# A two-layer perceiver kernel: its first loads split and reordered, and ScalarE's first instruction put ahead of its waits

## The reference, cut to what matters

```python
x = x + _L0_xattn_ref(_layernorm(x), ctx_1024, ctx_1024, ...)   # cross attention, 16 heads, causal
x = x + _L0_attn_ref(_layernorm(x), ...)                        # gated self attention with a position bias
x = x + _L0_ffn_ref(_layernorm(x), ...)                         # feed-forward with quantized weights and values
x = x + _L1_xattn_ref(_layernorm(x), ctx_1024, ctx_1024, ...)   # cross attention over all 257 context tokens
x = x + _L1_attn_ref(_layernorm(x), ...)                        # self attention with a line bias
x = x + _L1_ffn_ref(_layernorm(x), ...)                         # three-layer feed-forward
```

```python
def _L0_xattn_ref(queries, keys, values, Wq, bq, Wk, bk, Wv, bv, Wo, bo):
    q = (queries @ Wq.T + bq).reshape(N, L, H, -1)
    k = (keys @ Wk.T + bk).reshape(N, S, H, -1)
    v = (values @ Wv.T + bv).reshape(N, S, H, -1)
    sm = jnp.einsum('nlhd,nshd->nlhs', q, k) / math.sqrt(D)
    causal_mask = jnp.triu(jnp.ones((L, S), dtype=bool), k=1)
    sm = jnp.where(causal_mask[None, :, None, :], -jnp.inf, sm)
    sm = jax.nn.softmax(sm, axis=-1)
    attn = jnp.einsum('nlhs,nshd->nlhd', sm, v)
    return attn.reshape(N, L, H * D) @ Wo.T + bo
```

## Time and profile before

| what | us |
|---|---|
| median of three runs | 1635.74 (1635.74 to 1636.04) |
| the profiled execution | 1634.2 |
| its span, first to last instruction | 1632.4 |
| TensorE busy in the span | 1463.9 (90%) |
| VectorE / ScalarE / GpSimd busy | 897.7 / 712.2 / 498.9 |

### The profile page before, as it was taken

How to read it: one execution, slowest core, us unless ns; L and a number is a source line. 1 busy time by engine, 2 the same in 40 slices (tenths; PEclk the granted TensorE clock), 3 DMA queues, 4 the chain that set the end, 5 groups by cost and what they waited for, 6 DMA issues and landing times.

```text
span 1632.4 us, 32837 instructions
## 1 busy us (share of the span) xinstructions
PE 1463.9 (90%) x12556; PEld 1127.3 (69%) x12556; DVE 897.7 (55%) x1896; ACT 712.2 (44%) x1761; POOL 498.9 (31%) x693
## 2 busy tenths in 40 slices
PE   3998996991799999999996688789999999999999
PEld 3887774431677777777775466548877885886787
DVE  3898897488545555565655588734224323422332
ACT  3887775395535554555553455421212211221221
POOL 1445551001026865865553577500000000000000
PEclk9999999995999999999998799989999999999999
DMA  7000000000031161145110000013321440342230
GB/s 280 24 10 2 1 0 1 1 0 27 14 130 40 39 237 46 39 142 211 39 32 2 1 2 0 1 45 136 135 104 50 153 159 13 136 163 76 91 136 13
DMA packets 49500, 111.38 MB, mean 68 GB/s; under 512 B 4240, under 2 KB 6800, under 8 KB 46864
## 3 DMA queue, kind: packets, MB, share of 16 engines
q1 hardware_dynamic: 49424, 110.36, 19.3%
HBM read 99.86 MB, written 10.49 MB: 68 GB/s over the span
## 4 chain that ended last, share of the span: by engine, by line
PE 70%; DVE 15%; issue 6%; POOL 5%; ACT 2%; DMA 1%; SPq 0%; DVEq 0%; POOLq 0%; ACTq 0%
PE ps L843 22%; PE ps L491 15%; PE ps L695 6%; PE ps L497 6%; PE ps L689 5%; PE ps L894 3%; PE ps L715 3%; DVE R L1223 2%; PE ps L667 2%; DVE R L1519 2%; PE ps L726 2%; DVE amax L1392 2%; POOL R L1792 1%; POOL R L1810 1%; PE ps L560 1%
## 5 line engine op out<-in xcount | busy, mean ns | idle before, releaser
L843 PE MATMUL ps<-R 128*128 128x256 f32 x1792 | 388.6, 379 | 3.4 <-DVE R L1649 3.4
L843 PEld LDWEIGHTS ps<-R 128*128 128x128 f32 x1792 | 340.0, 190 | 52.2 <-issue 6.5
L491 PE MATMUL ps<-R 128*128 128x128 f32 (+1 forms) x1344 | 307.3, 388 | 6.4 <-DVE R L1388 4.8
L491 PEld LDWEIGHTS ps<-R 128*128 128x128 f32 x1344 | 190.5, 194 | 119.3 <-issue 109.6
L1792 POOL TENSOR_TENSOR R<-R,c_inv 128x1024 f32<-128x1024 f32 x64 | 121.1, 1893 | 170.4 <-DVE c_inv L1558 170.4
L1109 ACT ACTIVATE R<-ps,c_nmx 128x257 f32<-128x257 f32 x256 | 118.0, 474 | 112.0 <-DVE c_nmx L1543 112.0
L1519 DVE COPY R<-ps 128x512 f32<-128x512 f32 x128 | 88.2, 689 | 106.3 <-PE ps L715 105.1
L689 PE MATMUL ps<-R,x_wk 128*128 128x256 f32 x512 | 128.6, 394 | 0.8 <-POOL R L1784 0.8
L695 PE MATMUL ps<-x_wv,R 128*128 128x256 f32 x512 | 121.1, 379 | 0.0
L1870 POOL TENSOR_SCALAR g_ve<-g_mv 128x4 f32<-128x4 f32 x4 | 0.9, 236 | 345.6 <-DVE g_mv L1611 345.6
L689 PEld LDWEIGHTS ps<-R,x_wk 128*128 128x128 f32 x512 | 92.7, 191 | 17.9 <-POOL R L1784 1.4
(11 more groups left out here) (205 smaller groups left out, 2463.4 us busy)
## 6 DMA issues: line engine op xcount, KB each, us to landing
R<-quadrant_sums SPq DMA_DIRECT2D x32, 1024.0 KB, 6.8
R<-in_f_hq SPq DMA_DIRECT2D x32, 768.0 KB, 4.6
R<-in_ctxT SPq DMA_DIRECT2D x64, 257.0 KB, 2.7
R<-in_f_hq SPq DMA_DIRECT2D x8, 1024.0 KB, 8.3
quadrant_sums<-R SPq DMA_DIRECT2D x8, 1024.0 KB, 7.6
R<-in_f_w SPq DMA_DIRECT2D x3, 1024.0 KB, 7.1
R<-in_ctxk SPq DMA_DIRECT2D x16, 128.0 KB, 2.1
out<-x SPq DMA_DIRECT2D x4, 512.0 KB, 2.6
```

What stands on the lines that cost most here:

```text
L491: r = mm(dst, w[:, ki, fo * P:(fo + 1) * P], src[:, ki, :], start=(ki == 0), stop=(ki == KI - 1))
L843: r = mm(ps[:, 4 * (g % 2) + bk, half * HALF:(half + 1) * HALF], f_wr[g % 3][:, w, ki * P:(ki + 1) * P], src[:, k, ki, :], start=(ki == 0) ...
```

## The change

- The first load of `x` brings four tiles (512 KB, `x[:, 0:NL]`) and keeps the semaphore `in_x`; the other twelve (1536 KB) have a semaphore `in_x_rest`. VectorE's wait for `in_x` counts one load. In rounds 1 to 3 of X0 `d_norm` waits for `in_x_rest` and increments `passed` ahead of its statistics.
- The constants are loaded in the order `ident`, `colb`, `mask4`, `mask_hr`, `par` (`N_CONST = 5`). `causal` and `rowb` are loaded behind X0's weights and the first two pieces of context, with a semaphore `in_add`. `d_mask` in X0 and GpSimd's `bias` in X0 wait for it.
- ScalarE's first instruction is an activation of one column into a new buffer `act_start`, which waits for `consts_made` alone.
- `posmask_ready` and `pl_scale_ready` become one semaphore `later_made`; `passed` has no entry for ScalarE.

```diff
-            sp.dma_start(x[:, 0:2, :], A["x"][:, 0:2, :]).then_inc(in_x, 16)
-            for d, n in ((ident, "ident"), (par, "par"), (mask_hr, "mask_hr"), (mask4, "mask4"),
-                         (causal, "causal"), (colb, "colb"), (rowb, "rowb")):
+            sp.dma_start(x[:, 0:NL, :], A["x"][:, 0:NL, :]).then_inc(in_x, 16)
+            for d, n in ((ident, "ident"), (colb, "colb"), (mask4, "mask4"), (mask_hr, "mask_hr"), (par, "par")):
                 sp.dma_start(d[:], A[n]).then_inc(in_const, 16)
             for d, n in ((x0_wq, "x0_wq"), (x0_wk, "x0_wk"), (x0_wv, "x0_wv"), (x0_wo, "x0_wo")):
                 sp.dma_start(d, A[n]).then_inc(in_w["x0"], 16)
...
-            for l in range(NL):
-                load_ctxk(l, 0)
-            sp.dma_start(x[:, 2:T, :], A["x"][:, 2:T, :]).then_inc(in_x, 16)
+            load_ctxk(0, 0)
+            load_ctxk(1, 0)
+            for d, n in ((causal, "causal"), (rowb, "rowb")):
+                sp.dma_start(d[:], A[n]).then_inc(in_add, 16)
+            load_ctxk(2, 0)
+            load_ctxk(3, 0)
+            sp.dma_start(x[:, NL:T, :], A["x"][:, NL:T, :]).then_inc(in_x_rest, 16)
...
         @block.scalar
         def _(act):
-            for m in free["act"]:
-                act.sem_inc(m, 1)
             af = nc.scalar.activation
+            act.wait_ge(consts_made, 1)
+            af(act_start[:, :], minus_half[:, 0:1], ACT.Identity)
...
                 if kind == A0:
                     dve.wait_ge(s["x_updated"], tile(i, l))
                     stand(dve, "dve")
+                elif not isinstance(i, int):
+                    dve.wait_ge(in_x_rest, 16)
+                    stand(dve, "dve")
                 v.bn_stats(stats[l][:, :], xl[:, i, l, :]).then_inc(s["stats_ready"], 1)
...
             def d_mask(kind, l, i, n):
+                if kind == X0:
+                    dve.wait_ge(in_add, 32)
                 dve.wait_ge(s["scores_ready"], tile(n, l))
...
-            dve.wait_ge(in_x, 32)
+            dve.wait_ge(in_x, 16)
...
             def bias(l, i, n, k):
 
+                if k == BO0:
+                    pool.wait_ge(in_add, 32)
                 pool.wait_ge(s["xn_ready"], tile(n, l))
...
-            pool.wait_ge(pl_scale_ready, 2)
+            pool.wait_ge(later_made, 3)
```

More of the change, by code:

```diff
@@ L251, in perceiver @@
         magic = sb("magic", [P, 1])
+        act_start = sb("act_start", [P, 1])
         ps = ctx.enter_context(nc.psum_tensor("ps", [P, 8, 512], F32))
         in_const, in_later_const = sem("in_const"), sem("in_later_const")
-        in_x = sem("in_x")
+        in_x, in_x_rest, in_add = sem("in_x"), sem("in_x_rest"), sem("in_add")
         in_w = {k: sem(f"in_w_{k}") for k in ("x0", "a0", "nat", "x1", "a1", "ffn")}
-        posmask_ready, gate_bias_ready, pl_scale_ready, consts_made = map(
-            sem, ("posmask_ready", "gate_bias_ready", "pl_scale_ready", "consts_made"))
+        later_made, gate_bias_ready, consts_made = map(sem, ("later_made", "gate_bias_ready", "consts_made"))
         ctxk_in = lanes("ctxk_in")
@@ L275, in perceiver @@
         dve_link = sem("dve_link")
-        passed = {e: sem(f"{e}_passed") for e in ("act", "dve", "pool", "pe")}
+        passed = {e: sem(f"{e}_passed") for e in ("dve", "pool", "pe")}
         def after(eng, m, value):
@@ L317, in perceiver @@
         quad_in, quad_sum, quad_out = map(sem, ("quad_in", "quad_sum", "quad_out"))
-        free = {"act": (), "dve": (f0_x, g_ys), "pe": (g_xT,)}
+        free = {"dve": (f0_x, g_ys), "pe": (g_xT,)}
         F0_WEIGHTS = (1, 0, 2)
@@ L375, in perceiver @@
         BIAS_V = {X0: colb[:, BV0, :], A0: colb[:, BVA, :], A1: a1_bv[:, :]}
-        N_CONST, N_LATER_CONST = 7, 6
+        N_CONST, N_LATER_CONST = 5, 6
         xl = x[:, :, :].rearrange("p (i l) d -> p i l d", l=NL)
@@ L1355, in _ @@
                 v.tensor_scalar(qb[:, n, :], colb[:, at, :], 0.25, None, ALU.mult).then_inc(gate_bias_ready, 1)
-            dve.wait_ge(in_x, 32)
+            dve.wait_ge(in_x, 16)
             def enter_a0():
                 dve.wait_ge(in_later_const, 16 * N_LATER_CONST)
-                v.tensor_tensor(posmask[:, :], posmask[:, :], causal[:, :], ALU.add).then_inc(posmask_ready, 1)
-                v.tensor_scalar(plscale[:, :], plscale[:, :], 4.0, None, ALU.mult).then_inc(pl_scale_ready, 1)
-                dve.wait_ge(pl_scale_ready, 1)
+                v.tensor_tensor(posmask[:, :], posmask[:, :], causal[:, :], ALU.add).then_inc(later_made, 1)
+                v.tensor_scalar(plscale[:, :], plscale[:, :], 4.0, None, ALU.mult).then_inc(later_made, 1)
+                dve.wait_ge(later_made, 2)
                 v.tensor_tensor(plsc[:, :, :], plscale[:, :].unsqueeze(2).broadcast_to([P, H, NLINE]),
                                 plsign[:, :].unsqueeze(1).broadcast_to([P, H, NLINE]), ALU.mult)\
-                    .then_inc(pl_scale_ready, 1)
-                dve.wait_ge(posmask_ready, 1)
+                    .then_inc(later_made, 1)
+                dve.wait_ge(later_made, 1)
                 dve.wait_ge(in_w["nat"], 48)
```

## The result

| | before | changed |
|---|---|---|
| median of four runs, us | 1635.89 (1635.74 to 1636.49) | 1624.16 (1623.47 to 1628.45) |
| ratio | | 0.9933 [0.9916, 0.9951] |
| the profiled execution, its span | 1634.2, 1632.4 | 1628.45, 1626.5 |
| busy TensorE / VectorE / ScalarE / GpSimd | 1463.9 / 897.7 / 712.2 / 498.9 | 1471.1 / 898.6 / 713.1 / 498.4 |

The changed kernel is 11.7 us faster. The forecast was 1622.8, from 1619.8 to 1626.2. Note two things in the table. The runs of the changed kernel are 5 us apart where those of before were within 0.8. And TensorE is busy for 7.2 us longer though it does the same work. The profiled execution is the slowest of the four.

A forecast was written before the change was run, and what follows sets the result against it. The prediction took the head's chain from the load of x to the first matrix work as the bound: 11.6 us (x and constants) plus 1.3 (table load) gives 12.9, from 1635.74 to 1622.8 us, range 1619.8 to 1626.2.

The forecast's parts named there:

- The chain and its new start: Kernel head: from the load of x through VectorE, GpSimd and ScalarE; first transpose moves from 22.22 to 9.3 us.
- The term for `x` and the constants: VectorE's first statistics start at about 5.6 instead of 17.20: 11.6 us, 8.1 from x and 3.5 from constants.
- The table: ScalarE's table load ahead of the first a_scale leaves the path and runs during the first loads: 1.3 us.
- Tiles of `x`: First load of x, now 512 KB issued at 0.73, lands between 3.6 and 5.4, taken as 4.5; decides nothing.
- Weights: X0's four weights before the first transpose: the last lands at 8.4, 0.9 before 9.3, so costs nothing.
- Case (a): Rival: weights become the bound, TensorE starts at 10.4 to 11.4, about 1624.4 us; chance 0.12.
- What is late next: causal, rowb, the twelve tiles and round 1's context, wanted 12.9 us earlier, still land in time; tightest margin 3.4 us.
- Added waits: 28 more already-met waits on VectorE in X0: between 0 and 1.6 us, taken as 0.
- (b): Rival: TensorE's first half-rate stretch changes length by 16 passes, 1.8 us either way, 1621.0 or 1624.6; chance 0.10.
- (c): Rival: a drain as long as the table load leaves ScalarE's path too, start 1.3 us earlier, 1621.5; chance 0.02.
- (d): Rival: ScalarE's table load runs only with the waiting a_scale, 1.3 us lost, 1624.1; chance 0.03.
- (e): Rival: slower than before, TensorE staying at half rate through X0; 40 us longer would end at 1643; chance 0.01.

The follow-up runs named there:

- its own experiment: The changed kernel without its early one-column activation, so ScalarE's table load falls back in front of the first a_scale: 1626.08 us, ratio 0.9944.
- the kernel with late loads: The changed kernel with the loads for later blocks issued behind the context of round 1: 1624.99 us, ratio 0.9927.
- the best version: The changed kernel with added waits once in round 0, 20 unread products at the start and 28 unread transposes in the second block's idle time: 1619.50 us.
- the 28 transposes alone: The changed kernel plus 28 transposes nobody reads in TensorE's idle time in the second block, at about 245 us: 1623.09 us, ratio 0.9911.
- the shifted program: The changed kernel with ten semaphore increments more at the head of VectorE's program: 1624.72 us, ratio 0.9921.
- the waits once with 20 products: The changed kernel with added waits made once in round 0 and 20 unread matrix products at TensorE's start: 1623.96 us, ratio 0.9930.
- the kernel with only `x` split: The changed kernel with the seven constants in their old order and the table load late, keeping only the split load: 1627.93 us, ratio 0.9954.

## Why the prediction was right, point by point

**The chain and its new start: right.** Forecast 9.3, measured 9.68. The term for `x` and the constants was 11.6 and is 17.20 - 5.94 = 11.26; `par` landed at 3.08 + 2.55 = 5.63 instead of 5.2, because behind a load of 512 KB it took 2.5 us and not the 2.1 of the earlier trace rows. Within the term, the split of 8.1 for `x` and 3.5 for the constants measured 7.75 and 3.6. The table was 1.3, and is 1.28 in the sum, 1.20 by its own experiment. Together 12.54 of the 12.9.

**Tiles of `x`: right**, 4.0 us in bounds of 2.9 and 4.7, and not waited for.

**Weights: the right verdict on a wrong margin.** The last was to land at 8.4 and landed at 9.04 (issued at 4.98, 4.1 us). It landed at 9.87 in the kernel with late loads, where the start came at 9.96, and at 9.76 in the best version, where it was the releaser and the start came at 9.85. The step that failed is 0.8 us for each weight counted from a first one at 6.0: it landed at 6.41, and the last took another 2.6 instead of 2.4. The margin was 0.6, not 0.9, and the landings 0.7 and 0.8 later used it up. Case (a) is thus not refuted but at the edge, with a price of 0.2 to 0.3 where it occurred.

**What is late next: right.** `rowb` landed at 12.5 (12.9 forecast) and GpSimd stood for 2.17 us instead of 3.6, and nobody behind it. Round 1's context landed at 34.23, 0.2 later than the latest forecast, and was not waited for; neither was `causal`.

**Added waits: 0 for the waits was right, the term was still wrong.** I took 0 and gave 1.6 as the bound, at 0.057 us a wait. With the waits in and VectorE's program shifted they cost 0.1 us up to 100 us of before; in the changed kernel 1.1 is lost up to there. Of this, 0.7 is lost by the place at which the spread comes to stand in VectorE's program: the exclusion between VectorE and GpSimd makes 0.7 us out of 0.28. The step that failed is to price an inserted instruction by its own duration alone. The reason given for 0, that the chain there is TensorE's, was too coarse as well: 0.84 us of waiting for one spread of VectorE went straight into TensorE's start.

**(b), the clock: right in kind, too small in size, wrong in place.** I gave it 1.8 us either way at the start, and 1.0 at a second place. At the start it took 0.1 to 0.2. Further on is where most of it went: 1.5 us at 113 in all three profiles of the changed kernel, and 0.6 to 3.8 from 240 to 300. The list of slices in (b) has neither place: they are slices 4 and 7 of the earlier trace rows, the second busy for six tenths only, but with the granted clock at 9. At 113 TensorE waits 1.69 or 1.70 us for ScalarE in every one of the 14 profiles, before included, and the clock fell right behind it in six: three of the changed kernel, the 28 transposes alone, the shifted program, and the waits once with 20 products. That goes neither with the long spread nor with any edit, and stays open. "Three runs within 0.3 us speak against a large share of chance in it" is the step that failed: over the 32 later runs the kernel before itself took 1634.0 to 1638.9. Behind the idle time of 2.64 us the clock had fallen in nine of the ten profiles of kernels with an early start and no transposes there, in none of the three with them, and not in that of before. The tenth, at full clock, is the kernel with only `x` split. So the idle time is needed for the fall at this place, and isn't enough for it, since two kernels have the same one at full clock. What decides between the two was not found. Work placed in it removes that one fall; in all three kernels with it the next one came at 257 to 261 us.

The Trainium skill, "TensorE: Matmul & The Clock Gate", section "What's actually happening", says that how many matmuls are slow at a start is run-variable; the trace agrees: the kernels with the waits once and 20 products, with and without the 28 transposes, are the same program up to the second block, and their first projections took 4.57 and 2.94 us; those of the changed kernel took 4.58, 4.79 and 4.71.

**(c) falls:** with the table load gone from the path 1.20 to 1.28 us were saved, the load and nothing along with it. **(d) falls:** the load is at 0.73. **(e) falls** as a whole, though its mechanism, matmuls at half the clock, is the one that took most of what was lost.

**The sum.** 12.9 forecast, 11.7 measured as a difference of medians, and 5.9, 8.7 and 9.2 as the lead at the end of the three profiles. Less 0.4 at the start, less 1.1 for the spread and its place, less 1.5 and 0.6 to 3.8 for the clock. So part of the hit is luck. The losses that the sum left out were partly made up by the scatter of the medians: beside other runs of before the same kernel came to 1625.89 and 1626.81, which is 9.6 and 8.8 us below before instead of 11.7, and the last lies outside the forecast range of 1619.8 to 1626.2. The 12.54 at the first transpose is no luck; it came in each profile to 0.2 us.

## What to carry to other kernels

Load what the first round reads by itself, order the rest by first use, and put a one-column activation ahead of ScalarE's waits: the time to the first matmul is then a sum of rows that can be read beforehand, here to 0.4 us of 12.9. Whether it arrives at the end is decided elsewhere: behind one small idle time of TensorE deep in the program up to 3.8 of the 12.5 us were lost in clock, so compare leads at a dozen points of two traces, and try filling the idle times behind which the clock falls (with the waits once and 20 products this gave 4.5 us). And look at the rows around an edit for a single instruction that takes longer than its likes: ten idle increments at the head of the program took 1 us away here.

## What the runs showed of the hardware that was not expected

- An instruction of VectorE started 0.28 us late at one fixed place of its program, whatever the loads were doing, and ten semaphore increments ahead of it moved the delay to a queue instruction where it cost nothing. In the kernels with the identical VectorE program it was there each time, to 0.01 us.
- VectorE's spread (two inputs from the on-chip memory) and GpSimd's operations don't run at the same time: the one that came second took 1.80 instead of 1.16, or 1.04 instead of 0.19. So 0.28 us of delay cost TensorE 0.7.
- In one idle time of 2.64 us the clock fell in all three profiles of the changed kernel, and in that of the kernel before, with the same idle time, it didn't. What it cost differed from one execution to the next: 3.8, 0.7 and 0.6 us between 240 and 300 us of before.
